# Recurrent attention on one Trainium2 core: sends split over two queues, roots and squares on ScalarE, state operands laid out repeated

## The reference

```python
r, k, v = xr @ W_r, xk @ W_k, xv @ W_v
w_log = -softplus(-(w0 + tanh(xw @ w1) @ w2)) - 0.5
a = sigmoid(a0 + xa @ a1 @ a2)
g = sigmoid(xg @ g1) @ g2
kk = (k * k_k).reshape(B, T, H, N)
kk = kk / maximum(norm(kk, axis=-1, keepdims=True), 1e-12)
k = k * (1.0 + (a - 1.0) * k_a)
def step(state, inp):          # one time step, state is 8 x 8 per head
    sa = einsum('bhij,bhj->bhi', state, a_t)
    state = state * d_t[:, :, None, :] + sa[..., None] * b_t[:, :, None, :] + v_t[..., None] * k_t[:, :, None, :]
    return state, einsum('bhij,bhj->bhi', state, r_t)
o = group_norm_per_head(o) ; o = o + ((r * k * r_k).sum(-1) * v)
x = x + o * g @ W_o
x = x + square(relu(kf @ W_ffn1)) @ W_ffn2
```

## Time and profile before

| what | value |
|---|---|
| time, median of 3 runs | 5173.32 us (5163.14 to 5174.13) |
| profiled execution | 5184.22 us, span 5182.1 us |
| busy, share of the span | PE 76%, PEld 53%, DVE 52%, ACT 40%, POOL 19% |
| array building | 57 to 391 us, granted PE clock 0.74 |
| scan | 391 to 718 us, granted PE clock 0.98 |
| output stage | 718 to 961 us, granted PE clock 0.69 |

### The profile page before, as it was taken

One profiled execution on the slowest core, in us unless ns is written; L12 is line 12 of the kernel. 1 busy time (PEld: TensorE's weight loads), 2 busy tenths in 40 slices (PEclk: granted clock), 3 DMA queues, 4 the chain that ended last, 5 costly groups with the idle time before them and its releaser, 6 DMA issues. The chain is left out here.

```text
span 5182.1 us, 64858 instructions
## 1 busy us (share of the span) xinstructions
PE 3937.7 (76%) x19738; PEld 2738.9 (53%) x19800; DVE 2686.7 (52%) x6897; ACT 2047.1 (40%) x4136; POOL 1004.0 (19%) x970
## 2 busy tenths in 40 slices
PE   3548976699976688868886988897899877720498
PEld 1116644377753365646664766675577655520266
DVE  5758967322224676657774344333222255579444
ACT  3322111244433288858883344333333333300132
POOL 1000003100000376546651000000000001144200
PEclk9769987799987699989997999998999966655599
DMA  1440011000000000000000000000000000000000
GB/s 28 64 67 6 4 57 36 37 1 0 0 4 16 17 1 0 1 18 1 0 1 15 1 0 0 0 0 9 25 0 0 5 0 0 0 1 0 17 0 16
DMA packets 45619, 58.53 MB, mean 11 GB/s; under 512 B 14058, under 2 KB 37836, under 8 KB 44588
## 3 DMA queue, kind: packets, MB, share of 16 engines
q1 hardware_dynamic: 45484, 56.92, 4.7%
HBM read 34.87 MB, written 10.51 MB: 9 GB/s over the span
## 5 line engine op out<-in xcount | busy, mean ns | idle before, releaser
L418 PEld LDWEIGHTS bank<-moe_w,moe_hidden 128*128 128x128 f32 x5376 | 626.6, 192 | 78.5 <-issue 76.5
L418 PE MATMUL bank<-moe_w,moe_hidden 128*128 128x128 f32 x5376 | 630.3, 275 | 0.0
L408 PE MATMUL bank<-normed_t,moe_w 128*128 (+1 forms) x1344 | 615.8, 600 | 11.7 <-ACT moe_hidden L470 8.4
L546 DVE SCALAR_TENSOR_TENSOR branch<-bank,moe_weights,branch 128x128 f32<-128x128 f32 x768 | 216.4, 344 | 708.1 <-PE bank L418 704.0
L470 ACT ACTIVATE moe_hidden<-bank,moe_b 128x512 f32<-128x512 f32 x544 | 373.0, 687 | 505.5 <-PE bank L408 504.0
L90 POOL TENSOR_TENSOR branch_norm_shifted<-branch_norm_moments,eps 128x4 f32<-128x4 f32 x64 | 12.8, 200 | 1903.8 <-DVE branch_norm_moments L83 1903.8
L408 PEld LDWEIGHTS bank<-normed_t,moe_w 128*128 128x128 f32 x1344 | 245.0, 193 | 256.6 <-issue 240.4
L1465 DVE TENSOR_TENSOR ssm_mixer<-ssm_decay,bank 128x384 f32<-128x384 f32 x256 | 141.9, 554 | 301.0 <-PE bank L1151 263.3
L1960 POOL TENSOR_TENSOR local_size<-local_size,local_half_powers 128x8 f32<-128x8 f32 x128 | 257.2, 2009 | 201.5 <-DVE local_size L2026 197.5
L1281 ACT ACTIVATE ssm_decay<-bank 128x384 f32<-128x384 f32 x256 | 124.9, 491 | 327.3 <-PE bank L1132 327.2
L1664 PE MATMUL bank<-local_wqkv,local_shifted 128*128 128x512 f32 x384 | 209.5, 637 | 56.0 <-DVEq L2018 24.4
(11 more groups left out here) (532 smaller groups left out, 8966.8 us busy)
## 6 DMA issues: line engine op xcount, KB each, us to landing
rwkv_kept<-rwkv_keep SPq DMA_DIRECT2D x8, 768.0 KB, 18.5
moe_w<-in_moe_w_dram SPq DMA_DIRECT2D x2, 2304.0 KB
rwkv_gate<-rwkv_kept SPq DMA_DIRECT2D x8, 512.0 KB, 3.4
moe_w<-in_moe_w_dram SPq DMA_DIRECT2D x2, 2048.0 KB
...
```

What stands on the lines that cost most here:

```text
L408: pe.matmul(hbank[n % 4][:], w1[:, e, f * P:(f + 1) * P], source_t[:, bass.ds(i * PN, PN)], start=True, stop=True).then_inc(hidden_up, 1)
L418: last = pe.matmul(obank[e % 2][:, t * P:(t + 1) * P], hid[:, e % 2, f, t * P:(t + 1) * P], w2[:, e, f, :], start=(f == 0), stop=(f == chu ...
L546: last = dve.scalar_tensor_tensor(core.branch[:, t, :], obank[e % 2][:, t * P:(t + 1) * P], weights[:, i * PT + t, e - first_routed:e - fi ...
```

## The change

1. Array building. One semaphore per array and buffer parity (`landed`) takes the place of `arrays_in`, and `kept_in` is split by parity. Each consumer waits only for the array it overwrites. SP sends the decays and b when `products` is done with them, then r after `finish`, then the store of `keep`. ScalarE issues v of its own pair and w and k of the pair before on its own DMA queue, between the evict of g2 and the padding evict. ScalarE and VectorE loops are written out.
2. The head lengths are clamped from PSUM by VectorE behind `turn_rows` (`keep_lengths`), and ScalarE makes the inverse root as exp(-0.5 ln x). The reciprocal goes. The same for the root of the output stage.
3. Scan. `to_sa` and `to_out` hold each operand repeated for all 128 numbers of the state; VectorE makes `recalled` and `shown` in one instruction each; `stage` writes ten copies of 512 elements and three of 256.
4. Output stage. The squares of relu move from GpSimd to ScalarE.

The diff, cut to its core:

```diff
@@ rwkv_arrays @@
+        def send(queue, n, i, buffer):
+            for j in range(2):
+                b = 2 * i + j
+                queue.dma_start(home[n][b * GROUPS:(b + 1) * GROUPS, :, :],
+                                buffer[:].rearrange("p (j t) -> p j t", j=2)[:, j, :]).then_inc(landed[n][i % 2], 16)
-                sp.wait_ge(arrays_ready, i + 1)
-                for array, buffer in zip(arrays, (*sent[s], decay_two[s])):
-                    for j in range(2):
-                        b = 2 * i + j
-                        sp.dma_start(array[b * GROUPS:(b + 1) * GROUPS, :, :],
-                                     buffer[:].rearrange("p (j t) -> p j t", j=2)[:, j, :]).then_inc(arrays_in, 16)
+                sp.wait_ge(rates_ready, i + 1)
+                send(sp, "d", i, decay_two[s])
+                send(sp, "b", i, sent[s][4])
+                sp.wait_ge(recv_ready, i + 1)
+                send(sp, "r", i, sent[s][0])
                 sp.wait_ge(keep_ready, i + 1)
-                sp.dma_start(kept[i], keep[s][:]).then_inc(kept_in, 16)
-            sp.wait_ge(kept_in, 16 * PAIRS)
-            sp.wait_ge(arrays_in, 16 * 12 * PAIRS)
+                sp.dma_start(kept[i], keep[s][:]).then_inc(kept_in[s], 16)
...
+                def free(*names):
+                    if i >= 2:
+                        for n in names:
+                            act.wait_ge(landed[n][s], 32 * (i // 2))
                take("g1", bent_g[:], ACT.Sigmoid, low_ready[2])
-                if reused:
-                    act.wait_ge(arrays_in, (i - 1) * 16 * 12)
-                    act.wait_ge(kept_in, (i - 1) * 16)
-                if not (isinstance(i, int) and i == 0):
+                free("w")
+                if i > 0:
                     act.wait_ge(key_done, i)
                     act.wait_ge(lengths_used, i)
                 take("k", k_raw[:], ACT.Identity, k_ready,
                      more=((w[:], ACT.Identity, cols[:, 10:11]), (squares[:], ACT.Square, cols[:, 10:11])))
                 act.sem_inc(squares_ready, 1)
+                free("b")
                 take("a2", b[:], ACT.Sigmoid, a_ready, bias=cols[:, 9:10])
                 take("w2", decay[s][:], ACT.Sigmoid, bias=cols[:, 8:9])
+                free("r")
                 take("r", r[:], ACT.Identity)
-                take("v", v[:], ACT.Identity)
-                act.drain()
+                free("v")
+                take("v", v[:], ACT.Identity, values_ready)
                 act.activation(decay[s][:], decay[s][:], ACT.Exp, scale=-DECAY)
                 act.drain()
                 act.sem_inc(act_ready, 1)
+                if i >= 2:
+                    act.wait_ge(kept_in[s], 16 * (i // 2))
                 take("g2", keep[s][:, 1, :], ACT.Identity, g_ready)
-                if has_next:
+                act.wait_ge(values_ready, i + 1)
+                send(act, "v", i, v)
+                if i > 0:
+                    send_keys(i - 1)
+                if i < PAIRS - 1:
                     pad(i + 1)
-                act.wait_ge(lengths_up, i + 1)
-                act.activation(lengths[:], core.bank[LENGTHS][:], ACT.Sqrt).then_inc(lengths_ready, 1)
+                act.wait_ge(lengths_kept, i + 1)
+                act.activation(lengths[:], lengths[:], ACT.Ln)
+                act.drain()
+                act.activation(lengths[:], lengths[:], ACT.Exp, scale=-0.5).then_inc(lengths_ready, 1)
+            def send_keys(q):
+                act.wait_ge(keys_ready, q + 1)
+                send(act, "w", q, sent[q % 2][1])
+                send(act, "k", q, sent[q % 2][2])
...
-            def products(q, s, reused):
+            def products(q, s):
                 r, w, k, v, b = sent[s]
                 d = decay[s]
-                dve.wait_ge(lengths_ready, q + 1)
-                dve.tensor_scalar(lengths[:], lengths[:], 1e-12, None, ALU.max)
                 dve.wait_ge(act_ready, q + 1)
                 dve.tensor_tensor(with_k, k[:], r[:], ALU.mult)
-                dve.drain()
-                dve.reciprocal(lengths[:], lengths[:])
                 dve.tensor_tensor(even(decayed_r), even(d[:]), even(r[:]), ALU.mult)
-                if reused:
-                    dve.wait_ge(arrays_in, (q - 1) * 16 * 12)
+                if q >= 2:
+                    dve.wait_ge(landed["d"][s], 32 * (q // 2))
                 dve.tensor_tensor(decay_two[s][:], even(d[:]), odd(d[:]), ALU.mult)
                 dve.drain()
+                dve.wait_ge(lengths_ready, q + 1)
                 dve.tensor_tensor(w[:], w[:], lengths[:], ALU.mult).then_inc(lengths_used, 1)
...
+                dve.sem_inc(keys_ready, 1)
...
+            def keep_lengths(i):
+                dve.wait_ge(lengths_up, i + 1)
+                dve.tensor_scalar(lengths[:], core.bank[LENGTHS][:], 1e-24, None, ALU.max).then_inc(lengths_kept, 1)
...
@@ rwkv_scan @@
-        to_sa, to_out = isb("to_sa", [P, 2, CK, 3, PC]), isb("to_out", [P, 2, CK, 2, PC])
+        to_sa, to_out = isb("to_sa", [P, 2, CK, 3, ST]), isb("to_out", [P, 2, CK, 2, ST])
...
-                act.activation(to_sa[:, slot, :, 0:2, :], by_step(recall_w), ACT.Identity)
-                act.activation(to_sa[:, slot, :, 2, :], decays[:, :, m * CK:(m + 1) * CK].rearrange("p x c -> p c x"),
-                               ACT.Identity)
+                def spread(out, array):
+                    for h in range(PH):
+                        act.activation(out[:, :, h * HD * HD:(h + 1) * HD * HD].rearrange("p c (i j) -> p c i j", j=HD),
+                                       array[:, h * HD:(h + 1) * HD, :].rearrange("p j c -> p c j").unsqueeze(2)
+                                       .broadcast_to([P, CK, HD, HD]), ACT.Identity)
+                steps = lambda array, s: array[:, :, at].rearrange("p x (c s) -> p x c s", s=2)[:, :, :, s]
+                for s in range(2):
+                    spread(to_sa[:, slot, :, s, :], steps(recall_w, s))
+                spread(to_sa[:, slot, :, 2, :], decays[:, :, m * CK:(m + 1) * CK])
+                for s in range(2):
+                    spread(to_out[:, slot, :, s, :], steps(recv, s))
                 act.activation(rows_of[:, slot, :, 0:2, :], by_step(rates), ACT.Identity)
                 act.activation(rows_of[:, slot, :, 2:4, :], by_step(keys), ACT.Identity)
-                act.activation(values_of[:, slot], by_step(values), ACT.Identity)
-                act.activation(to_out[:, slot], by_step(recv), ACT.Identity).then_inc(staged, 1)
+                act.activation(values_of[:, slot], by_step(values), ACT.Identity).then_inc(staged, 1)
...
-                    for h in range(PH):
-                        lane = slice(h * HD * HD, (h + 1) * HD * HD)
-                        shape = [P, 3, HD, HD]
-                        now = dve.tensor_tensor(
-                            recalled[:, s, :, lane].rearrange("p a (i j) -> p a i j", j=HD),
-                            state[:, lane].rearrange("p (i j) -> p i j", j=HD).unsqueeze(1).broadcast_to(shape),
-                            to_sa[:, slot, k, :, h * HD:(h + 1) * HD].unsqueeze(2).broadcast_to(shape), ALU.mult)
-                    now.then_inc(recalled_ready, 1)
+                    dve.tensor_tensor(recalled[:, s], state.unsqueeze(1).broadcast_to([P, 3, ST]), to_sa[:, slot, k],
+                                      ALU.mult).then_inc(recalled_ready, 1)
...
+                    now = dve.tensor_tensor(shown[:, slot, k], state.unsqueeze(1).broadcast_to([P, 2, ST]),
+                                            to_out[:, slot, k], ALU.mult)
...
@@ rwkv_out @@
-                act.activation(spread[:], core.bank[0][:], ACT.Sqrt, bias=cols[:, 4:5]).then_inc(rooted, 1)
+                act.activation(spread[:], core.bank[0][:], ACT.Ln, bias=cols[:, 4:5])
+                act.drain()
+                act.activation(spread[:], spread[:], ACT.Exp, scale=-0.5).then_inc(rooted, 1)
...
-                act.wait_ge(hidden_done, i * HC)
+                if has_tail:
+                    act.wait_ge(out_up, i)
                 for f in range(HC):
                     act.wait_ge(hidden_up, i * HC + f + 1)
                     act.activation(relu[:, f, :], core.bank[2 + f][:], ACT.Relu).then_inc(relu_done, 1)
+                    if f > 0:
+                        act.drain()
+                        act.activation(hidden[:, f - 1, :], relu[:, f - 1, :], ACT.Square).then_inc(hidden_done, 1)
+                act.drain()
+                act.activation(hidden[:, HC - 1, :], relu[:, HC - 1, :], ACT.Square).then_inc(hidden_done, 1)
...
-                pool.wait_ge(out_up, i)
-                for f in range(HC):
-                    pool.wait_ge(relu_done, i * HC + f + 1)
-                    pool.tensor_tensor(hidden[:, f, :], relu[:, f, :], relu[:, f, :], ALU.mult).then_inc(hidden_done, 1)
...
-                dve.reciprocal(spread[:], spread[:])
```

79 lines of the change are left out of this document (38 added, 41 removed).

## The result

The changed kernel took 5114.1 us in the median of its runs (5104.1 to 5120.2) against 5173.7 (5163.1 to 5176.6): a ratio of 0.9887, interval 0.9865 to 0.9908. Run again as a control it was at 0.9857 (0.9837 to 0.9876). The forecast was 5104 in 5083 to 5140, a ratio of 0.9866. The profiled execution took 5120.15 us, its span was 5118.4, that is 63.7 less than before; the forecast for it was 69.6.

What follows compares the result with a forecast made beforehand. Took VectorE's chain, once the DMA wait is gone, to bound array building. Terms of -57.2 there, -0.2 scan and -12.2 output made -69.6 us: 5114.6 for the profiled execution, 5104 for the median, range 5083 to 5140.

Steps and rivals of the forecast that it cites:

- The wait and the pair period: Array building: without ScalarE's wait for the store of `keep`, pairs 2 to 6 go from 37.25 to 30.85 us.
- I take SP's quick price: Array building: ScalarE's six sends between g2 evict and padding cost 3.9 us, at SP's 1.26 for two transfers.
- rival 1: Array building: issuing on ScalarE costs as on a backed-up SP, six sends 6.8 us instead of 3.9; 5124, chance 0.18.
- The last pair and the drain: End of array building: last pair -10.7 us; drain before the scan -13, bounds -9 and -16.
- the step from 9 to 13: Drain before the scan: 13 us saved at 109 GB/s, 9 at 80 GB/s, where one queue ran.
- The scan: Scan stage: 128 steps shorter by 0.065 us, -8.3; bare staging before the first step +8.1; sum -0.2 us.
- The root's price of 2.0: Output stage: logarithm, drain, load and exponential ahead of padding delay `delta` by 2.0 us, seven times, +14.
- What follows is built alike, so its price is nothing: Blocks behind the output stage: same code in both kernels, so no change in time, 0 us.
- 2: Array building's DMA: engines stay as with one queue, or rate dips to 70 GB/s; drain 4 us longer; 5115, chance 0.1.
- 3: Output stage: second FFN matmuls start at TensorE's 1.2 GHz again, +1.6 us six times; 5114, chance 0.12.
- 4: Array building: `w` queues behind `v` on ScalarE, the take still waits, 32 us lost in pairs 2 to 6; 5136, chance 0.06.
- 5: Scan: ScalarE's staging becomes the bound, spreads of 2.1 us or more, kernel slower; 5172 to 5190, chance 0.04.

Runs made afterwards that it cites:

- sends_on_sp: The changed kernel with v, w and k sent by SP's queue, each array on its own semaphore: 5106.9 us, ratio 0.9859 to the kernel before.

## Why the prediction was right

- **The wait and the pair period.** Forecast 30.85, measured 31.09, by two errors that nearly cancel. The step "I take SP's quick price" was sized too low: six sends took 4.5 to 6.1 us (pairs 1 to 6, mean 5.0), between its 3.9 and the 6.8 of rival 1. But of their time more was hidden than I thought: the g2 evict now comes early enough that in three pairs of six padding still waits for the transposes (the row of 34.1 us, whose longest, 18.9, is the first pair's), and the sends ahead of it cost nothing there (30.10, 29.59 and 29.66, where one queue has 30.12, 29.62 and 29.68). That the two sizes cancelled was luck; the bound by VectorE and the path through padding were right. VectorE's own chain is 28.5 us (31.31 less the 2.76 of idling).
- **The last pair and the drain.** `w` scaled 43.3 us earlier, forecast 44.2; then 14.8 instead of 13 won, inside the bounds. I took the step from 9 to 13 from a second queue. With one queue (sends_on_sp) the drain is 28.8, so 13.0 of the 14.8 came without it: what counts is that the arrays leave earlier.
- **The scan.** Start +8.2 against 8.1: ten spreads at 1.0 on the empty chip. Steps -8.9, or -7.3 by the other executions named above, where -8.3 was forecast. Ratio 1.0008: by itself no gain.
- **The output stage.** The root's price of 2.0 held (2.57 against 0.59), and `branch` moved by 3.9 of the 4.2 forecast. The stretch from first `delta` to last `branch` gave 3.4 more than forecast, spread thinly: 1.0 in the first interval between deltas (22.78 to 23.81, forecast +2.0), 1.5 in the next five (together -12.5, forecast -11), 0.5 in the last (-4.7, forecast -4.2) and 0.4 in the last `branch`. Up to the first `delta` I had 0.7 and it was 1.8, since the variance matmuls ahead of its logarithm ran at the lower clock (2.07 us, 1.13 before).
- **The later blocks.** "What follows is built alike, so its price is nothing" was too simple: 12.2 us in the routers, which kernels with the old and with the new output stage show in one profile and not in another. Up to the last `branch` the stages had gained 73.0, where 69.6 were forecast for all; the routers and the rest took 9.3 back.
- **Rivals.** 1 was right that issues next to SP's own cost more (up to 2.70 for two), but six never took its 6.8, and half of the pairs covered them: its 5124 did not come. 2 was right in its rule (116 and 117 GB/s) and wrong in the loss that I worked out from it, a drain 4 us longer: with one queue it was 1.8 longer, since `w` and `k` leave earlier there too. 3 did not come: the second FFN matmuls took 3.83. 4 and 5 fell: no transfer was waited for, a spread takes 1.09.
- **What the forecast did not ask** is whether each part of the change was worth having. By the marks three were not: the second queue, the root by logarithm in the output stage and where it stands, and, until its first block is shared, the repeated operands. The logarithm in array building and the semaphores without the rest were not run by themselves.
- **The median.** 5104 was forecast, 5114 and then 5108 measured. That the total came so near is in part chance, since it holds 12 us of the routers in the profile and a scatter of as much between executions; the marks up to the last `branch` carry the forecast.
